# Sorting network of a graph kernel: the two words of each record are compared by one VectorE operation instead of one each

## The reference

```python
h = jnp.maximum(_layernorm(x, axis=-1), 0.0)
for t in range(2):
    messages = concatenate([h[dst], h[src], edge_weight], 1) @ msg_W[t].T + msg_b[t]
    agg = segment_sum(messages, src, num_segments=N)
    h = _gru_cell(agg, h, gru_Wih[t], gru_bih[t], gru_Whh[t], gru_bhh[t])
return x + h
```

## Time and profile before

| | |
|---|---|
| median of 3 runs | 2413.81 us (2413.45 to 2416.66) |
| profiled execution | 2400.32 us, its span 2398.8 us |
| TensorE clock, mean | 0.979 of full speed |
| VectorE busy | 2192.0 us (91%) |
| ScalarE busy | 1963.7 us (82%) |
| TensorE busy | 1621.8 us (68%) |
| sorting, from first to last compare operation | 61.0 to 599.5 us |

### The profile page before, as it was taken

How to read it: one execution, slowest core, us unless ns; L and a number is a source line. 1 busy time by engine, 2 the same in 40 slices (tenths; PEclk the granted TensorE clock), 3 DMA queues, 4 the chain that set the end, 5 groups by cost and what they waited for, 6 DMA issues and landing times. The chain is left out here.

```text
span 2398.8 us, 126601 instructions
## 1 busy us (share of the span) xinstructions
PE 1621.8 (68%) x47260; PEld 1529.0 (64%) x47260; DVE 2192.0 (91%) x3766; ACT 1963.7 (82%) x4390; POOL 612.9 (26%) x853
## 2 busy tenths in 40 slices
PE   0000000000138899999999999968999999999996
PEld 0000000000138899999999999858999999999996
DVE  6999999999369899999999999868999999999995
ACT  3776895563158899999999999868999999999996
POOL 1000000000633344454554444401211111211121
PEclk9999999999968999999999999989999999999998
DMA  5100001110426666666666666556766777677773
GB/s 105 41 0 0 0 0 38 45 22 21 124 49 228 211 226 224 232 228 227 227 228 227 226 231 225 176 193 202 238 235 233 243 233 239 235 243 233 237 237 116
DMA packets 175418, 400.70 MB, mean 167 GB/s; under 512 B 73071, under 2 KB 76789, under 8 KB 174855
## 3 DMA queue, kind: packets, MB, share of 16 engines
q1 hardware_dynamic: 116907, 204.17, 27.0%
q0 software_dynamic: 57296, 195.19, 24.4%
q10 hardware_dynamic: 1132, 0.27, 0.1%
HBM read 384.63 MB, written 14.57 MB: 166 GB/s over the span
## 5 line engine op out<-in xcount | busy, mean ns | idle before, releaser
L1200 ACT ACTIVATE rows<-ps_rows 128x512 f16<-128x512 f32 x2744 | 1454.4, 637 | 66.9 <-PE ps_rows L1123 44.3
L1140 PE MATMUL ps_sum<-rows,src 128*64 128x132 f16 (+1 forms) x21952 | 1153.3, 225 | 15.0 <-ACT rows L1200 9.4
L1140 PEld LDWEIGHTS ps_sum<-rows,src 128*64 128x64 f16 x21952 | 905.1, 142 | 26.8 <-ACT rows L1200 18.6
L1293 DVE TENSOR_TENSOR src<-iota_units,src_lane 128x2048 f16<-128x2048 f16 (+1 forms) x784 | 863.3, 1101 | 42.7 <-PE ps_sum L1140 42.6
L1123 PE MATMUL ps_rows<-rows_next,dst 128*64 128x128 f16 x10976 | 547.9, 220 | 37.2 <-DVE dst L1284 22.3
L1123 PE MATMUL ps_rows<-rows_now,dst 128*64 128x128 f16 x10976 | 546.1, 220 | 22.2 <-DVE dst L1284 10.3
L1284 DVE TENSOR_SCALAR dst<-lanes,lane_no 128x2048 f16<-128x2048 f16 (+1 forms) x784 | 533.0, 680 | 4.2 <-DMA lanes<-lanes_dram 3.6
L862 PE MATMUL ps_src<-ident,late 112*64 112x112 f32 x98 | 29.9, 337 | 627.0 <-DVE taken L934 626.4
L1123 PEld LDWEIGHTS ps_rows<-rows_next,dst 128*64 128x64 f16 x10976 | 413.0, 111 | 60.4 <-issue 26.9
L1123 PEld LDWEIGHTS ps_rows<-rows_now,dst 128*64 128x64 f16 x10976 | 412.9, 111 | 45.3 <-issue 15.9
L862 PEld LDWEIGHTS ps_src<-ident,late 112*64 112x64 f32 x98 | 14.6, 149 | 629.7 <-DVE taken L934 627.3
(11 more groups left out here) (188 smaller groups left out, 2052.6 us busy)
## 6 DMA issues: line engine op xcount, KB each, us to landing
lanes<-lanes_dram POOLq DMA_DIRECT2D x294, 512.0 KB, 4.8
lanes<-lanes_dram SPq DMA_DIRECT2D x294, 512.0 KB, 4.7
lanes<-lanes_dram POOLq DMA_DIRECT2D x98, 256.0 KB, 4.1
lanes<-lanes_dram SPq DMA_DIRECT2D x98, 256.0 KB, 4.1
rows_now<-parts_dram SPq DMA_DIRECT2D x112, 32.0 KB, 1.7
rows_next<-parts_dram SPq DMA_DIRECT2D x112, 32.0 KB, 3.6
parts_dram<-rows_now SPq DMA_DIRECT2D x1, 3136.0 KB, 16.2
sorted_dram<-planes SPq DMA_DIRECT2D x1, 3136.0 KB, 11.6
```

What stands on the lines that cost most here:

```text
L1140: last = nc.tensor.matmul(ps_sum[b][at, 0:width], hot[:, at], row, start=(j == 0), stop=(j == J - 1))
L1200: nc.scalar.activation(rows[:, (u + NU * b) % ring, 0:n, 0:2 * H], cut(ps_rows[(u + NU * b) % 4][:])[:, 0:n, :], ACT.Copy).then_inc(rows_r ...
L1293: nc.vector.tensor_tensor(src1[q][:, 0:len(units)], iota_units[:].rearrange("p (o l) k -> p o l k", o=1) .broadcast_to([P, len(units), P, ...
```

## The change

The two words become the outermost free dimension of every operand. `dst_i` and the sorting half of `attr_room` are replaced by one buffer `second_room` of two planes, as `planes` and `late` are already. Each compare step has one `min` and one `max` over both words, each ScalarE copy carries both words, and there is one semaphore `passed` and one `carried`. To make space, `beyond` moves into `attr_room`, and the GRU's weights and biases of the preparation move into `rows_now`.

```diff
-        dst_i = sb("dst_i", [P, SORTED], I32, scope=sort_scope)
+        second_room = sb("second_room", [P, 2, SORTED], scope=sort_scope)
+        dst_i = second_room[:, 0, :].bitcast(I32)
...
-        beyond = sb("beyond", [P, EW], BF16, scope=sort_scope)
+        beyond = attr_room[:, EW:EW + EW // 2].bitcast(BF16)
...
-        wih = sb("wih", [H, 3, ROUNDS, H], scope=prep_scope)
-        whh = sb("whh", [H, 3, ROUNDS, H], scope=prep_scope)
+        wih, whh = [rows_now[:].rearrange("p c f -> p (c f)").bitcast(F32)[0:H, k * G * ROUNDS:(k + 1) * G * ROUNDS]
+                    .rearrange("p (g r f) -> p g r f", g=3, r=ROUNDS) for k in range(2)]
...
-        here = [planes[:, v, 0:SORTED] for v in range(2)]
-        there = [dst_i[:].bitcast(F32), attr_room[:, 0:SORTED]]
+        here, there, late_rooms = planes[:, :, 0:SORTED], second_room[:], late[:]
...
-            return t.rearrange("p (c x) -> p c x", x=run)[:, at // run:at // run + 2 * blocks - 1:2, :]
+            return t.rearrange("p v (c x) -> p v c x", x=run)[:, :, at // run:at // run + 2 * blocks - 1:2, :]
...
                 for ops, moves in stages():
...
-                    if ops[0][0] == LAST_STEP:
-                        for v in range(2):
-                            act.wait_ge(passed[v], 2 * steps_done)
-                            act.wait_ge(carried[v], moves_done[v])
-                    for v in range(2):
-                        wait(act, passed[v], 2 * steps_done)
-                        wait(act, carried[v], moves_done[v])
-                        for source, target in moves[v]:
-                            nc.scalar.activation(target, source, ACT.Copy).then_inc(carried[v], 1)
-                        moves_done[v] += len(moves[v])
+                    wait(act, passed, 2 * steps_done)
+                    wait(act, carried, moves_done)
+                    for source, target in moves:
+                        nc.scalar.activation(target, source, ACT.Copy).then_inc(carried, 1)
+                    moves_done += len(moves)
...
-                        for v, (low, high, low_to, high_to) in enumerate(places):
-                            wait(dve, carried[v], moves_done[v])
-                            wait(dve, passed[v], 2 * steps_done)
-                            nc.vector.tensor_tensor(low_to, low, high, ALU.min).then_inc(passed[v], 1)
-                            nc.vector.tensor_tensor(high_to, low, high, ALU.max).then_inc(passed[v], 1)
+                        low, high, low_to, high_to = places
+                        wait(dve, carried, moves_done)
+                        wait(dve, passed, 2 * steps_done)
+                        nc.vector.tensor_tensor(low_to, low, high, ALU.min).then_inc(passed, 1)
+                        nc.vector.tensor_tensor(high_to, low, high, ALU.max).then_inc(passed, 1)
```

More of the change, by code:

```diff
@@ L290, in count_below @@
             wait(nc.scalar, counts_ready, m)
-            nc.scalar.activation(beyond[:], src_i[:], ACT.Sign, bias=below[:, m:m + 1],
+            nc.scalar.activation(beyond, src_i[:], ACT.Sign, bias=below[:, m:m + 1],
                                  accum_out=balance[:, m:m + 1]).then_inc(counts_ready, 1)
@@ L485, in build @@
         pads_ready = sem("pads_ready")
-        passed = [sem(f"passed{v}") for v in range(2)]
-        carried = [sem(f"carried{v}") for v in range(2)]
+        passed = sem("passed")
+        carried = sem("carried")
         pads_out = sem("pads_out")
@@ L555, in stages @@
                 for place, reach, blocks, run in stage:
-                    ops.append((n, blocks * run, [[f(t[v], at, blocks, run) for f, t in ((in_order, now), (put, to)) for at in (place, place + reach)]
-                                                  for v in range(2)]))
+                    ops.append((n, blocks * run, [f(t, at, blocks, run) for f, t in ((in_order, now), (put, to)) for at in (place, place + reach)]))
                     n += 1
-                yield ops, [[(in_order(now[v], *left), put(to[v], *left)) for left in left_in_order(stage)] for v in range(2)]
+                yield ops, [(in_order(now, *left), put(to, *left)) for left in left_in_order(stage)]
                 now = to
@@ L564, in stages, with put @@
                 to, other = other, now
-                def put(v, *where):
-                    return in_pairs_at(v, *where) if last else in_residues(to[v], *where)
+                def put(*where):
+                    return in_pairs_at(*where) if last else in_residues(to, *where)
                 ops = []
@@ L571, in stages @@
                     at = [(low, 0, run), (high, shift, run)]
-                    ops.append((n, len(range(4)[low]) * run, [[in_residues(now[v], *where) for where in at] + [put(v, *where) for where in at]
-                                                              for v in range(2)]))
+                    ops.append((n, len(range(4)[low]) * run, [in_residues(now, *where) for where in at] + [put(*where) for where in at]))
                     n += 1
-                yield ops, [[(in_residues(now[v], *left), put(v, *left)) for left in left_in_residues(stage)] for v in range(2)]
+                yield ops, [(in_residues(now, *left), put(*left)) for left in left_in_residues(stage)]
                 now = to
-        late_rooms = [late[:, v, :] for v in range(2)]
         WIDE = [n for ops, _ in stages() for n, width, _ in ops if width >= 1024]
@@ L645, in stray_job @@
                         act.wait_ge(counts_ready, EARLY)
-                        nc.scalar.activation(beyond[:], lane_i, ACT.Relu, bias=limits[:, 0:1],
+                        nc.scalar.activation(beyond, lane_i, ACT.Relu, bias=limits[:, 0:1],
                                              accum_out=stray[:, 0:1]).then_inc(stray_ready, 1)
@@ L649, in stray_job @@
                         act.wait_ge(stray_ready, 1)
-                        nc.scalar.activation(beyond[:], lane_i, ACT.Relu, scale=-1.0,
+                        nc.scalar.activation(beyond, lane_i, ACT.Relu, scale=-1.0,
                                              accum_out=stray[:, 1:2]).then_inc(stray_ready, 1)
@@ L653, in stray_job @@
                         act.wait_ge(stray_ready, 2)
-                        nc.scalar.activation(beyond[:], attr_in, ACT.Relu, bias=limits[:, 1:2],
+                        nc.scalar.activation(beyond, attr_in, ACT.Relu, bias=limits[:, 1:2],
                                              accum_out=stray[:, 2:3]).then_inc(stray_ready, 1)
@@ L657, in stray_job @@
                         act.wait_ge(stray_ready, 3)
-                        nc.scalar.activation(beyond[:], attr_in, ACT.Relu, bias=limits[:, 1:2], scale=-1.0,
+                        nc.scalar.activation(beyond, attr_in, ACT.Relu, bias=limits[:, 1:2], scale=-1.0,
                                              accum_out=stray[:, 3:4]).then_inc(stray_ready, 1)
@@ L747, in _ @@
                 dve.wait_ge(pads_ready, 2)
-                steps_done, moves_done = 0, [0, 0]
+                steps_done, moves_done = 0, 0
                 for ops, moves in stages():
@@ L752, in _ @@
                         dve.wait_ge(low_ready, 2)
[L753 to L756, removed]
                     for n, _, places in ops:
```

21 lines of the change are left out of this document (11 added, 10 removed).

## The result

The changed kernel is slower. Its median is 2421.84 us (22 runs) against 2413.11 us of the kernel before on the same chip (22 runs); the ratio over all these runs is 1.0028 with a 95% interval of 1.0016 to 1.0041, that is +6.8 us (3.9 to 9.9); the two medians alone are 8.7 us apart. The forecast was no change, 2413.8 us, with a range up to 2420, and the measured median lies above that range.

The account below looks back on a forecast made before the run. VectorE, busy throughout the sort, was taken to bound the kernel. The terms -11.2, +6.7, +4.8 and -0.3 summed to 0.0 us, so the median was forecast as 2413.8 us, range 2407 to 2420.

Parts of the forecast that it names:

- Part 2: Borders between sort stages: each stage waits for its own last operation, 64 x 0.105 = +6.7 us.
- Part 1: VectorE in the sort: merging 320 operations into 160 saves 0.07 us of fixed cost each, -11.2 us.
- Part 3: Nine narrow sort stages: VectorE waits for ScalarE's copies, which now all begin with the stage, +4.8 us.
- Parts 4 and 5: Last sort stage loses its separate stop, -0.3 us; moving `beyond`, weights and biases costs 0.
- The sign by the sort's end: The sort should end within 2 us of 599.5; off by more than 5 us makes the prediction wrong.
- Rival A: Stage borders: the dependence is free, total -6.7 us, 2407.1 us; chance 0.11.
- Rival B: Merged operations: the third free dimension costs one element time per row step, 25.6 us, 2439 us; chance 0.07.
- Rival C: ScalarE holds up more than the nine stages; 4.8 us needs 0.53 us more per narrow stage; chance 0.12.

Follow-up runs that it names:

- e1: Changed kernel with `passed` and `carried` made one semaphore, so each compare operation waits for one count; sort 540.05 us, ratio to the kernel before 1.0003.
- e2: Changed kernel with VectorE's two waits swapped, first `passed`, then `carried`; sort 540.75 us in its one execution, no ratio.
- e5: Changed kernel with words compared apart in narrow stages and those ahead of them, operations and copies sharing semaphores; sort 538.2 us, ratio to the kernel before 1.0016.
- e4: Kernel before with only the moves of memory, words still compared and copied apart; sort 538.5 us, ratio to the kernel before 0.9999.
- e7: Changed kernel with ScalarE's two waits swapped, `carried` first, then `passed`; sort 544.5 us in its one execution, no ratio.
- e3: Changed kernel with two more waits, met long before, ahead of each compare step; sort 547.9 us in its one execution, no ratio.

## Why the prediction was wrong, by its steps

- **Part 2, the border, is the step that failed.** The mechanism was right (each stage now waits for its own last operation), the size was not: 0.105 us after the end and 0.08 before it make 0.185, not 0.105 in all; 64 x 0.185 = 11.8 us instead of 6.7. The rows that I took the price from the earlier trace rows have one wait ahead of the operation, the compare steps have two, and the late one stands second, as an instruction of its own. e1 and e2 show that with one wait, or the late one first, the 0.035 of the earlier trace rows holds. I had named the upper end, 0.26 from the earlier trace rows, and with it 16.6 us, but gave the range only half of it.
- **Part 1** was forecast as -11.2. The starts show it directly: from the first to the second operation of a step it is 0.059 us less, in the mean of the 80 steps, than the same distances of the two words together before, and 160 times that is 9.5. Solving for it in the changed kernel gives 5.5 - 11.8 - 3.6 + 0.3 = -9.6, and in e1 1.5 - 64 x 0.115 - 4.2 + 0.3 = -9.8: 0.06 us an operation instead of the rounded 0.07.
- **Part 3, the narrow stages:** forecast +4.8, measured 7 x (0.34 + 0.08) + 2 x (0.24 + 0.08) = 3.6. Place and cause were right (e5 takes the gaps away), the number was 1.2 us too high. Half of that is part 2 again: the late border lets VectorE start 0.07 us behind ScalarE's copies, so it waits less for them (in e1, without this, the same sum gives 4.2). The rest is that three copies took 3.80 us instead of 3.84, and that VectorE saw the last one after 0.03, not 0.05. Elsewhere ScalarE was late without harm, as forecast.
- **Parts 4 and 5:** -0.3, and 0 for the layout (e4: 0.9999).
- **The sum** with the measured terms is -9.5 + 11.8 + 3.6 - 0.3 = 5.6 us, and the sort is 5.5 longer. On the median that the forecast started from that is 2419.4, inside its range; the measured ratio makes it 2420.6 (2417.7 to 2423.7), and the measured median is 2421.84. Which part of the 1.2 us and more between them is noise stays open.
- **The sign by the sort's end** would have misled: it ended at 600.3, within the 2 us that I gave it, because this execution's sort began 4.7 us early. That is luck; by its length it is 5.5 us off.
- **Rival A** (a free dependence): no run agrees. With one wait the next operation starts 0.03 us after the end, without a dependence 0.08 us before it. I had taken rival A's rule from the Trainium skill, "VectorE: DVE Perf Modes", "The DRAIN you can't avoid", which says that a semaphore after each of eight copies cost nothing extra, and I read more into it than it states. It doesn't say whether its copies waited for each other. Here every compare operation raises a semaphore, and where none is waited for late that costs nothing, as there; it is the late wait that costs. The same section also says that a following operation that is not held starts earlier, and the 0.08 us before the end agree with that. **Rival B** (the third dimension): in stage 7, which has it, the two operations are 1.68 us apart against 1.67 by the formula, so at most 0.01 us an operation (in stage 6, where only the inputs have it, 3.81 against 3.80). **Rival C**: nine gaps, no more.

## What to carry to other kernels

Two interleaved chains on one engine hide each other's semaphore latency; merging them into operations of twice the size saves one fixed cost for each pair (here 0.06 us) and uncovers one latency for each dependent step (0.115 to 0.185 us), so it pays only where more than two to three operations are saved for each border (here 160 for 77). With the cheaper wait that part alone gained here (9.5 us against 64 x 0.115 = 7.4), and the waits for ScalarE behind the narrow stages took it back. When an operation must wait for two semaphores, wait first for the one that will be late. And a price for a wait has to be read from a row with the same number and order of waits.

## What the runs showed that I had not expected

- With two waits ahead of an operation, the late one costs 0.035 us as the first and 0.10 us as the second, on VectorE (e2) and on ScalarE (e7), whether it comes from the same engine or from another (narrow stages: 3.86 us against 3.94). With a single wait it is 0.035 (e1), with four and the late one last 0.13 (e3). The second wait is the dear one because it is an instruction of its own (0.021 us, or 0.017 on ScalarE) with 0.045 us behind it; met early, it costs nothing.
- The start of the sort differs between executions by up to 7 us (55.8 to 62.5), and the part behind it by up to 16 us (1798.4 to 1814.0), by 14.5 us for the changed kernel alone; the length of its sort repeats to 0.1 us (544.01, 543.95, 544.01). For a change inside it, one profile says more than the times of 20 runs.
